# State-space tables from TensorE outer products, their products on GpSimd, and another merged step order

## The chip, the cores and the metric

One core of a Trainium2 chip runs the whole program. The metric is the device time of one execution in microseconds. Three timed runs of the kernel before took 551.61, 553.63 and 553.75 us; the median is 553.63.

## The reference

The input is `x`, four batches of 512 tokens with 128 features. One layer is computed for each batch, in four parts.

1. Cross attention with 16 heads of 8 over a context of 77 keys, with an output projection and a residual sum.
2. A mixture of 8 experts (128 to 512 to 128, ReLU). A router picks two experts for each token, but all eight are computed and the unused ones weigh zero.
3. A text block: four heads of scores over the 77 keys, of which only the 32 largest of each row are kept (top-32), a softmax on those, a FiLM scale and shift made from the result, a state-space convolution over the 512 tokens (S4D), a second FiLM and a feed-forward part.
4. An 8-bit quantised 128 by 128 product with residual sum at the end.

The S4D convolution needs a kernel K of 512 time steps for each of the 128 channels. It does not depend on `x`:

```python
dt = exp(log_dt);  A = A_re + 1j*A_im;  dtA = dt[:, None] * A
dC = C * (exp(dtA) - 1) / A
powers = exp(dtA[:, :, None] * arange(L))
K = 2 * einsum('dn,dnl->dl', dC, powers).real        # 128 channels, 64 states
y = irfft(rfft(x) * rfft(K))[:L] + x * D_skip
```

## The kernel before

Everything is float32 except a few bf16 pieces of the attention scores. Every engine walks one list, `order`, and executes its own part of each step in that order. Semaphores join the engines. `order` is made in `plan()` from eleven streams of steps and the string `ORDER`, a hand-stored merge: each letter names a stream, with a repeat count. The streams: S setup, H attention and router of batches 0 to 3, K the S4D kernel tables, F FiLM weights, E expert products (`moe_up`, `moe_down`), C the sums of expert outputs (`moe_add`), U and T the text block, O the convolution, feed-forward and quantisation, Z the second half of that for the last batch, W warming matmuls that compute nothing needed. The E steps of a batch can start once its normalised tokens are transposed (`norm_T` of `moe`). The text block of a batch starts after its expert sums, and the last batch's text block has no expert products left beside it.

PSUM has eight banks. Four belong to the experts (`moe_h`, `moe_y`). The other four, `side`, are handed out in turn by `place_fills` in the order of the list, so a product cannot start until the reader of the fourth fill before it has emptied that bank. From the first to the last step of an attention group, its accumulator holds one of the four, and three rotate.

The stream K builds the tables of K. Partitions are 64 states, twice (real and imaginary); time is split as l = 32a + c, with a in 0..15 and c in 0..31.

- `kgen_base` 0 (VectorE, L1525 to L1539) makes the per-channel decay and angle, `ar`, `r`, `u32`, `a32`. `kgen_base` 1 (L1543 to L1569, with a Tanh and two Sin on ScalarE) makes the coefficients `p1` and `p2`.
- The channels then go in four groups of 32. For group i, `kgen_ang` (VectorE, L1577 to L1584) makes the angles 32a, sine and cosine, as a broadcast product and range reductions by adding and subtracting a large number, on 128x512 elements. `kgen_rot` (L1589 to L1592) does the same for the angles c on 128x1024. `kgen_sin` is three Sin on ScalarE.
- `kgen_exp` is two broadcast products on GpSimd (L1756, L1757) and two Exp on ScalarE, into the single buffers `G1d` and `G2c`.
- `kgen_mul` is five products or sums on VectorE (L1598 to L1603), `t1` to `t4` on 512 columns and `tab` on 1024.
- `kgen_mm` is 32 small matmuls on TensorE (L1023), waiting for `tab`; ScalarE copies the result.

After the fourth group `kgen_dft` transforms K. The first step that needs the result belongs to the text block of batch 0. `setup_used` makes VectorE and GpSimd wait for early setup data, whose memory the tables overlay.

Other names: `attn_norm` (L872 on TensorE; reciprocal L1322 and product L1324 on VectorE), `o_proj` (L879, sum L1328), the LayerNorm steps `ln_stats` (L1276 to L1283, reciprocal root on GpSimd L1640) and `ln_apply` (L1293), `score` and `pv` (L850, L854, L865, exponential L1112), `smax` (L834, L1311), `topk` (L1384 to L1394) and `topw`.

Of the kernel before, what the change touches and what calls it, by code (L numbers as in the profile page):

```python
# [7 lines left out]
ALU = mybir.AluOpType  # L8
# [49 lines left out]
C_COLS = [("ident", 128), ("spread", HG * HD0), ("sign", 1), ("cosoff", 1), ("sinoff", 1), ("p1sign", 1), ("cvec", CC), ("avec", CA),  # L58
          ("half", 2), ("rest", NM), ("rest_on", NM), ("ones", 2)]
# [141 lines left out]
S H2 S H5 K H2 K W2 F2 W2 F W2 F W6 F H3 K H K2 H2 W K H2 K H18 K8 H W K H2 K H2 K3 H E10 H E6 H2 K E2 K H C2 K E6 K  # L201
E4 H C H2 E3 H E K2 C H E H E2 K2 E7 C E2 H2 E H C E H E3 H E C E H E2 C E4 H E2 C E U E7 C H E3 U H2 U H14 U H2 T H
C H2 E T H E5 T E5 H E C E7 H E C H C H E T E2 H E3 H2 E C2 E H E2 U3 H3 E11 C H T2 U T E H E3 C H T2 E3 C H2 E5 T
E3 T C T E H E4 H E2 H E3 C H E2 H C E2 U H E T E T3 E7 H2 T E H U T C T H3 T E H E H9 C H E T H T H2 T4 H E H2 T E6
C2 T H E4 O H U H2 E4 H E2 C H E H E3 H U C E2 U O E7 U H C E H T2 C O T E10 H2 E2 H O E O C E T E3 O2 U C U E U E2
H E U E T E H2 O C H U T3 E O2 E H E C E5 C E H E O E H T E4 T H E4 C2 E H E3 T E T E6 C T2 H E H E2 C E H2 T H E U
H2 E H E T E2 T7 H O E H3 T H2 E2 H E2 T H3 E H C E2 O E T H O E T H2 C2 T U2 O E H E3 U O E2 U E3 T H C E9 O T H E
C2 E T H2 T2 E6 C E8 O H2 C2 E H E O H T E T E2 H E5 T U O2 C U E12 O C E U2 E T O U T U T2 C E T4 E C O E2 T E5 T5
E2 T O2 C O T E11 C2 E8 T E C E3 O E2 T E T O E3 T C O E O E2 C O2 E U2 E2 C U E3 U E4 O E T E C T O E O E7 C O T O
E5 C O E T E C T O C U3 T4 U O T2 W U T7 O T O U T6 W O W T3 W O6 W7 O3 Z O Z W Z2 O2 Z O Z O3 Z2 O W2 Z2 O Z2 O Z O  # L210
Z
# [129 lines left out]
def plan():  # L341
# [3 lines left out]
    for run in ORDER.split():  # L345
        name = run[0]
        for _ in range(int(run[1:] or 1)):
# [12 lines left out]
         "dft": 2, "idft": 1, "ffn_up": HC, "ffn_down": 1, "quant_T": 1, "quant_mm": 1, "kgen_mm": 1, "kgen_dft": 2}  # L360
# [4 lines left out]
def place_fills(order):  # L365
# [13 lines left out]
    for kind, b, i in order:  # L379
# [8 lines left out]
        if kind == "attn_sum":  # L388
# [20 lines left out]
G_ACT = ["dt", "th", "sh", "sb"] + [(n, i) for i in range(ND) for n in ("s1", "s2", "s3", "e1", "e2")]  # L409
# [6 lines left out]
def recurrent_layers(nc, x, w1, w2, wpack, vpack, cpack, rpack, gpack, r2pack, xpack, vctx, dftf, dfti, b2, tmask, vmask, out):  # L416
# [10 lines left out]
    with ExitStack() as ctx:  # L427
# [7 lines left out]
        AREA = 13440  # L435
# [1401 lines left out]
```

## Time and profile before

| | |
|---|---|
| median of three timed runs | 553.63 us |
| profiled execution | 553.78 us, span 552.0 us |
| TensorE matmul busy | 478.6 us (87%), 2883 instructions |
| VectorE busy | 430.9 us (78%) |
| ScalarE busy | 264.7 us (48%) |
| GpSimd busy | 117.0 us (21%) |
| mean granted TensorE clock | 0.933 of full speed |
| the chain that ended last | 70% PE, 22% VectorE, 3% ScalarE, 2% GpSimd |
| first expert product (L910) starts; last expert product ends | 102.9 us; 468.0 us |
| last expert sum (L1370) starts | 469.65 us |

The span runs from the first to the last instruction; the execution's own time is 1.8 us longer. Busy shares are averages over stages that have different limits. The chain is followed back from the last instruction, at each step to what released it, so that its shares say which engine the end depended on. A matmul's end is modelled from a pipeline, and neighbouring ones overlap by some tenths of a microsecond; in the chain that overlap is taken out. The granted clock of TensorE has two levels here, 2.4 GHz (1.00) and 1.2 GHz (0.5); a mean between them is a mixture.

### The profile page before, as it was taken

The numbers are of one execution on the slowest core, as the hardware profiler recorded it, in microseconds if no ns is written. First come the engines' busy times: TensorE is split into PE (matmuls) and PEld (weight loads), VectorE is DVE, ScalarE is ACT, GpSimd is POOL, SyncE is SP. The second block draws the span as 40 slices with busy tenths as digits, with TensorE's granted clock in tenths as the row PEclk, the third lists the DMA queues.
The fourth block names the chain that finished last, engine by engine and source line by source line (L and its number), as shares of the span: only waits on it lengthen the run. The fifth ranks groups of instructions, "written<-read, shape, count | busy, mean of one in ns | idle before, by whom it ended". The sixth has DMA issues, their size and how long they took to land.

```text
span 552.0 us, 8986 instructions
## 1 busy us (share of the span) xinstructions
PE 478.6 (87%) x2883; PEld 370.6 (67%) x2883; DVE 430.9 (78%) x1781; ACT 264.7 (48%) x549; POOL 117.0 (21%) x198
## 2 busy tenths in 40 slices
PE   4386586799999999999999999999999999736971
PEld 3154234598975989848987985689878989514760
DVE  4378988885625787886797988899898789998667
ACT  4441466575456465564538456534474544411040
POOL 4522003122020031003015210310222331232021
PEclk9998595699999999999999999999999999956996
DMA  7900770002100004000003000000000000000000
GB/s 182 173 2 0 222 220 0 2 1 39 21 2 2 1 1 58 4 1 1 2 0 51 9 4 1 2 20 0 2 2 1 2 20 1 1 1 0 21 0 19
DMA packets 16176, 15.03 MB, mean 27 GB/s; under 512 B 1210, under 2 KB 14274, under 8 KB 16130
## 3 DMA queue, kind: packets, MB, share of 16 engines
q1 hardware_dynamic: 16130, 14.47, 11.7%
q8 instruction: 23, 0.38, 0.3%
q14 instruction: 23, 0.19, 0.1%
HBM read 9.15 MB, written 1.05 MB: 18 GB/s over the span
## 4 chain that ended last, share of the span: by engine, by line
PE 70%; DVE 22%; ACT 3%; issue 3%; POOL 2%; DMA 1%; DVEq 0%; POOLq 0%; ACTq 0%
PE moe_h L910 20%; PE moe_y L922 20%; PE side L865 5%; PE side L970 3%; PE side L980 2%; PE side L958 2%; DVE area L1394 2%; PE moe_h L932 2%; PE side L1001 2%; PE side L772 2%; DVE TOP L1384 1%; PE side L944 1%; PE side L989 1%; PE side L834 1%; PE side L1023 1%
## 5 line engine op out<-in xcount | busy, mean ns | idle before, releaser
L1132 ACT ACTIVATE HT<-moe_h,W 128x256 f32<-128x256 f32 x256 | 115.5, 473 | 104.0 <-PE moe_h L910 103.8
L910 PE MATMUL moe_h<-xnT_moe,W 128*128 128x256 f32 x512 | 138.0, 387 | 0.8 <-ACT HT L1132 0.7
L922 PEld LDWEIGHTS moe_y<-W,HT 128*128 128x128 f32 x1024 | 131.3, 192 | 8.8 <-issue 3.2
L922 PE MATMUL moe_y<-W,HT 128*128 128x128 f32 x1024 | 134.9, 276 | 0.0
L910 PEld LDWEIGHTS moe_h<-xnT_moe,W 128*128 128x128 f32 x512 | 88.3, 193 | 17.8 <-issue 7.2
L1370 DVE SCALAR_TENSOR_TENSOR X<-moe_y,RW,X 128x128 f32<-128x128 f32 x128 | 38.9, 346 | 8.1 <-PE moe_y L922 7.1
L865 PE MATMUL side<-PT,VP 128*72 128x512 f32 x80 | 43.1, 625 | 1.2 <-ACT PT L1112 1.2
L1394 DVE MATCH_REPLACE8 area<-TOP,area 128x77 f32<-128x77 f32 x192 | 40.9, 230 | 0.0
L932 PE MATMUL moe_h<-W 128*128 128x256 f32 x112 | 31.7, 436 | 0.0
L1384 DVE MAX8 TOP<-area 128x8 f32<-128x77 f32 x192 | 31.5, 230 | 0.0
L1704 POOL TENSOR_TENSOR area<-area 128x128 f32<-128x128 f32 x16 | 7.4, 463 | 110.3 <-ACT area L1155 110.3
L932 PEld LDWEIGHTS moe_h<-W 128*128 128x128 f32 x112 | 24.6, 223 | 9.2 <-issue 5.7
L1112 ACT ACTIVATE PT<-side 128x512 f32<-128x512 f32 x40 | 23.3, 594 | 13.5 <-PE side L850 10.6
L1311 DVE TENSOR_REDUCE mx<-side 128x6 f32<-128x462 f32 (+1 forms) x48 | 24.8, 580 | 5.7 <-PE side L834 5.6
L1384 DVE MAX8 TOP<-side 128x8 f32<-128x77 f32 x64 | 10.8, 231 | 17.4 <-PE side L945 17.3
L958 PE MATMUL side<-FF,AMT 78*128 78x512 f32 x32 | 19.4, 693 | 4.2 <-ACT AMT L1149 4.2
L1146 ACT ACTIVATE area<-area 128x308 f32<-128x308 f32 x16 | 7.4, 460 | 30.6 <-DVE area L1387 30.6
L834 PE MATMUL side<-KM,QA 96*128 96x154 bf16 x128 | 12.3, 237 | 10.5 <-DMA QA<-Q 9.8
L865 PEld LDWEIGHTS side<-PT,VP 128*72 128x72 f32 x80 | 11.1, 150 | 13.3 <-issue 8.2
L834 PEld LDWEIGHTS side<-KM,QA 96*128 96x128 bf16 x128 | 9.6, 100 | 14.8 <-DMA QA<-Q 11.4
L850 PE MATMUL side<-QA,KM 128*128 128x512 bf16 x32 | 12.7, 410 | 7.8 <-issue 6.8
L1756 POOL TENSOR_TENSOR area<-area,C 128x512 f32<-128x512 f32 x4 | 4.2, 1054 | 68.8 <-PE side L1023 51.8
(323 smaller groups left out, 851.8 us busy)
## 6 DMA issues: line engine op xcount, KB each, us to landing
W<-in_w SPq DMA_DIRECT2D x8, 512.0 KB, 7.7
QA<-Q SPq DMA_DIRECT2D x24, 128.0 KB, 4.4
X<-in_x SPq DMA_DIRECT2D x4, 256.0 KB, 6.5
KM<-area SPq DMA_DIRECT2D x6, 160.0 KB, 5.9
out_dram<-FO SPq DMA_DIRECT2D x3, 256.0 KB, 2.3
V<-in_vpack SPq DMA_DIRECT2D x1, 579.0 KB, 7.7
area<-in_r2pack SPq DMA_DIRECT2D x1, 576.0 KB, 8.0
area<-in_gpack SPq DMA_DIRECT2D x1, 576.0 KB, 8.5
```

The costliest lines, as they stand in the source:

```text
L834: mm = pe.matmul(dst[:, o:o + 2 * NK], QA[0:ZROWS, j, i * P:(i + 1) * P], KM[0:ZROWS, j, b, 0:2 * NK], start=True, stop=True)
L865: mm = pe.matmul(dst[0:GROWS, :], VP[:, g, n, :], PT[:, i % NPT, :], start=(n == 0), stop=(n == NG - 1))
L910: pe.matmul(moe_h[n % 2][:, 0:HS], W1[:, e, c * P:(c + 1) * P], xnT_moe[:, b % 2, h * HS:(h + 1) * HS], start=True, stop=True).then_inc(mo ...
L922: mm = pe.matmul(moe_y[m % 2][:, t * P:(t + 1) * P], HT[:, m % 2, c, t * P:(t + 1) * P], W2[:, e, c, :], start=(c == 0), stop=(c == HC - 1))
L932: pe.matmul(moe_h[n % 2][:, 0:HS], W[:, 0:P], W[:, 0:HS], start=True, stop=True)
L958: pe.matmul(dst[:], AMT[:, i % 2, :], FF[:, b, :], start=True, stop=True).then_inc(full, 1)
L1112: act.activation(PT[:, i % NPT, :], src[:], ACT.Exp).then_inc(read, 1)
L1132: act.activation(HT[:, m % 2, c, :], moe_h[n % 2][:, 0:HS], ACT.Relu, bias=wc("b1")[:, e * HC + c:e * HC + c + 1]).then_inc(moe_h_ready, 1)
L1311: dve.tensor_reduce(mx[:, i, :].rearrange("p (u j) -> p j u", u=2)[:, 3 * n:3 * n + pairs, :], src[:, 0:heads * NK].rearrange("p (j u k) - ...
L1370: ins = dve.scalar_tensor_tensor(X[:, b, t, :], moe_y[m % 2][:, k * P:(k + 1) * P], RW[:, b % 2, t, e:e + 1], X[:, b, t, :], ALU.mult, ALU ...
L1384: dve.max(TOP[:, a, h, r, :], s).then_inc(top_max, 1)
L1394: dve.match_replace(TW[:, h, :], TOP[:, a, h, r, :], s, PICKED)\
```

## The change

The broadcast products leave VectorE and GpSimd. A new step `kgen_T` transposes `u32`, `r`, `a32` and `ar` on TensorE into one bank, and ScalarE copies it to `UT`. A constant matrix `ES` (32 rows, 512 columns with a and 1024 with c, block diagonal over the 32 channels of a group) is loaded four times, by four DMAs on SyncE, behind `gpack`. The angles and exponents of a group are then products of 32 rows of `UT` with `ES` into PSUM: one matmul of 512 columns for `kgen_ang`, two for `kgen_rot`, three for `kgen_exp`. VectorE rounds straight from PSUM in four operations of 512 columns for `kgen_ang` and four for `kgen_rot`; the Sin takes a negative scale and a bias column. The Exp reads PSUM, as one operation for `G1d` and two for `G2c`. The five operations of `kgen_mul` run on GpSimd. They wait for `p2`, the Sin and the Exp. TensorE's `kgen_mm` now waits for GpSimd; VectorE's `kgen_ang` and `kgen_rot` of groups 2 and 3 wait for GpSimd's `t4` and `tab` of the group two before.

`kgen_base` 1 moves behind the first group's Sin in stream K. `ORDER` is another merge throughout: 82 steps stand before the first `moe_up` in both. Between the first `moe_up` and the last `moe_down` stand 754 steps before and 755 after: `kgen_rot` of group 3, and `topk` (1, 0), `topw` 0 and `text_n4` 0 of the last batch come in, and `ln_stats`, `ln_apply` and `norm_T` of `ffn` of batch 2 go behind the last `moe_down`. `topk` (1, 1) of the last batch now also stands before the last `moe_add`.

```diff
+    out = [("kgen_base", 0, 0), ("kgen_T", 0, 0)]
     for dh in range(ND + 1):
         if dh < ND:
             out += [("kgen_ang", 0, dh), ("kgen_rot", 0, dh), ("kgen_sin", 0, dh)]
+        if dh == 0:
+            out.append(("kgen_base", 0, 1))
...
-S H2 S H5 K H2 K W2 F2 W2 F W2 F W6 F H3 K H K2 H2 W K H2 K H18 K8 H W K H2 K H2 K3 H E10 H E6 H2 K E2 K H C2 K E6 K
+S H2 S H5 W5 K F3 K H3 W F2 H K3 W4 H2 K2 W4 H6 K H11 K H6 K8 H K2 H3 K H E4 H K4 H E2 K H E4 K H E H E C H E7 H K E
...
+            for g in range(ND):
+                sp.dma_start(ES[DH * g:DH * (g + 1)], epack).then_inc(e_in, 16)
...
+                if kind == "kgen_T":
+                    dst, full = free_for(pe, kind, b, i)
+                    pe.wait_ge(g_dve, GD["a32"])
+                    for n, k in enumerate(("u32", "r", "a32", "ar")):
+                        mm = pe.transpose(dst[:, n * P:(n + 1) * P], ga[k][:], ident)
+                    mm.then_inc(full, 1)
+                if kind in ("kgen_ang", "kgen_rot", "kgen_exp"):
+                    g = slice(DH * i, DH * (i + 1))
...
+                    for n, (k, c) in enumerate({"kgen_ang": ((0, 0),), "kgen_rot": ((1, 1), (1, 2)),
+                                                "kgen_exp": ((2, 0), (3, 1), (3, 2))}[kind]):
+                        dst, full = free_for(pe, kind, b, i, n)
+                        pe.matmul(dst[:], UT[g, k * P:(k + 1) * P], ES[g, c * 512:(c + 1) * 512], start=True, stop=True,
+                                  tile_position=(DH * i, 0)).then_inc(full, 1)
                 if kind == "kgen_mm":
-                    pe.wait_ge(g_dve, GD["tab", i])
+                    pe.wait_ge(g_pool, GP["tab", i])
...
                 if kind == "kgen_exp":
-                    act.wait_ge(g_pool, GP["m1", i])
-                    act.activation(G1d[:], G1d[:], ACT.Exp).then_inc(g_act, 1)
-                    act.wait_ge(g_pool, GP["m2", i])
-                    act.activation(G2c[:], G2c[:], ACT.Exp).then_inc(g_act, 1)
+                    if i == 0:
+                        setup_used(act)
+                    if i >= 1:
+                        k, m = FILL[("kgen_mm", 0, i - 1, 0)]
+                        act.wait_ge(side_full[k], m + 1)
+                    src, read = filled(act, kind, b, i, 0)
+                    act.activation(G1d[:].rearrange("p d a -> p (d a)"), src[:], ACT.Exp).then_inc(read, 1)
+                    for n in range(2):
+                        src, read = filled(act, kind, b, i, n + 1)
+                        act.activation(G2c[:].rearrange("p d c -> p (d c)")[:, n * 512:(n + 1) * 512], src[:], ACT.Exp).then_inc(read, 1)
...
                 if kind == "kgen_ang":
...
+                    if i >= 2:
+                        dve.wait_ge(g_pool, GP["t4", i - 2])
+                    src, read = filled(dve, kind, b, i)
+                    dve.tensor_scalar(G1b, src[:], cc("cosoff"), ROUND, ALU.add, ALU.add).then_inc(g_dve, 1)
+                    gelem(("y1", i), dve.tensor_scalar(G1c, src[:], cc("sinoff"), ROUND, ALU.add, ALU.add))
+
+                    dve.scalar_tensor_tensor(G1b, G1b, ROUND, src[:], ALU.subtract, ALU.subtract).then_inc(g_dve, 1)
+                    dve.scalar_tensor_tensor(G1c, G1c, ROUND, src[:], ALU.subtract, ALU.subtract).then_inc(read, 1)
...
-                if kind == "kgen_exp":
-                    a32 = ga["a32"][:, DH * i:DH * (i + 1)].unsqueeze(2).broadcast_to((P, DH, CA))
...
-                    gelem(("m1", i), pool.tensor_tensor(G1d[:], a32, av, ALU.mult))
-                    gelem(("m2", i), pool.tensor_tensor(G2c[:], a1, cv, ALU.mult))
+                if kind == "kgen_mul":
...
+                    pool.wait_ge(g_dve, GD["p2"])
+                    pool.wait_ge(g_act, GA["s2", i])
+                    gelem(("t1", i), pool.tensor_tensor(G1b[:], G1b[:], p1, ALU.mult))
+                    gelem(("t2", i), pool.tensor_tensor(G1c[:], G1c[:], p2, ALU.mult))
+                    gelem(("t3", i), pool.tensor_tensor(G1b[:], G1b[:], G1c[:], ALU.add))
+                    for n in range(3):
+                        emptied(pool, "kgen_exp", 0, i, n)
+                    gelem(("t4", i), pool.tensor_tensor(G1d[:], G1d[:], G1b[:], ALU.mult))
+                    gelem(("tab", i), pool.tensor_tensor(G2c[:], G2c[:], G2b[:], ALU.mult))
```

## Rows read from the trace of the kernel before

**Rows 1.** Stages (window, its length, busy us with instructions per engine; granted clock; DMA).

```profile
47.00:82.00 35.00, 22.27 (x135) 9.41 (x133) 32.42 (x48) 16.43 (x26) 2.96 (x2) 0.76 0.57 174
82.00:103.00 21.00, 12.32 (x99) 9.36 (x97) 17.49 (x28) 12.14 (x21) 6.97 (x5) 0.51 0.00 0
103.00:135.00 32.00, 31.18 (x284) 26.42 (x285) 22.10 (x57) 22.85 (x47) 6.10 (x10) 0.95 0.02 4
135.00:468.00 333.00, 333.00 (x2059) 270.12 (x2058) 267.64 (x1258) 176.63 (x391) 65.09 (x119) 1.00 0.06 10
468.00:504.00 36.00, 20.92 (x77) 12.05 (x76) 33.88 (x211) 10.57 (x24) 11.56 (x19) 0.74 0.00 1
504.00:552.00 48.00, 30.47 (x147) 23.42 (x146) 31.30 (x106) 7.87 (x16) 7.83 (x11) 0.86 0.04 12
```

**Rows 2.** Chain that ended last, 80 to 99 us (start us, us, what).

```profile
80.01 2.15 PE side L1023 x64
...
83.78 3.37 DVE qr L1322
...
94.30 1.05 POOL rstd_moe L1640
...
95.38 3.71 DVE xn_head L1293 x4
```

**Rows 3.** VectorE timeline (start us, us, engine, line): first coefficient operation, and what follows them.

```profile
36.51 0.22 DVE L1543 TENSOR_SCALAR area<-area 128x128 f32<-128x128 f32 x1
...
44.80 0.29 DVE L1514 TENSOR_REDUCE area<-area 128x1 f32<-128x128 f32 x1
```

**Rows 4.** VectorE timeline: one round of angles, rotations and products.

```profile
60.76 0.69 DVE L1577 TENSOR_TENSOR area<-area,C 128x512 f32<-128x512 f32 x1
...
61.49 0.49 DVE L1579 TENSOR_SCALAR area<-area,C 128x512 f32<-128x512 f32 x1
...
64.91 1.23 DVE L1589 TENSOR_TENSOR area<-area,C 128x1024 f32<-128x1024 f32 x1
...
68.94 0.69 DVE L1598 TENSOR_TENSOR area<-area 128x512 f32<-128x512 f32 x1
...
73.11 0.69 DVE L1577 TENSOR_TENSOR area<-area,C 128x512 f32<-128x512 f32 x1
```

**Rows 5.** ScalarE timeline: first score exponential, last copy of attention, a table load.

```profile
63.13 1.08 ACT L1112 ACTIVATE PT<-side 128x512 f32<-128x512 f32 x2
...
79.26 0.59 ACT L1118 ACTIVATE qs<-side 64x512 f32<-64x512 f32 x1
...
84.26 1.28 ACT L1179 ACT_TABLE_LOAD   x1
```

**Rows 6.** PE: 128x512 float32 product in the chain, 34 to 104 us.

```profile
38.52 0.86 PE side L807 x2
```

**Rows 7.** PE timeline of the scores: such a product at the lower clock.

```profile
66.04 1.91 PE L865 MATMUL side<-PT,VP 128*72 128x512 f32 x2
```

**Rows 8.** VectorE timeline: a sum that reads 512 columns of PSUM.

```profile
91.94 0.69 DVE L1328 TENSOR_TENSOR X<-side,X 128x512 f32<-128x512 f32 x1
```

**Rows 9.** GpSimd timeline beside the LayerNorm of the chain.

```profile
95.70 1.05 POOL L1756 TENSOR_TENSOR area<-area,C 128x512 f32<-128x512 f32 x1 [0.36 <-PE side L1023]
...
96.83 1.91 POOL L1757 TENSOR_TENSOR area<-area,C 128x1024 f32<-128x1024 f32 x1
```

**Rows 10.** GpSimd, the line of a plain 128x512 sum: ns min/median/max.

```profile
L1670 POOL TENSOR_TENSOR FO<-FO,xn_out x3: 1270/1272/1272, 362.8 to 511.1; 128x512 f32<-128x512 f32 x3
```

**Rows 11.** VectorE timeline: the same LayerNorm line with GpSimd idle.

```profile
122.96 1.12 DVE L1293 TENSOR_SCALAR xn_head<-X,mv_attn,rstd_attn 128x128 f32<-128x128 f32 x4 [0.68 <-POOL rstd_attn L1640]
```

**Rows 12.** VectorE timeline, top-32 rounds of the last batch.

```profile
472.60 0.67 DVE L1384 MAX8 TOP<-side 128x8 f32<-128x77 f32 x4
...
474.55 0.65 DVE L1384 MAX8 TOP<-area 128x8 f32<-128x77 f32 x4
...
475.94 0.65 DVE L1384 MAX8 TOP<-area 128x8 f32<-128x77 f32 x4
```

More of the change, by code:

```diff
@@ L359 @@
          "score": 1, "attn_norm": 1, "o_proj": 1, "router": 1, "w_T": 1, "b2_add": 1, "text_q": 1, "topk": 1, "am_T": 1, "film": 1,
-         "dft": 2, "idft": 1, "ffn_up": HC, "ffn_down": 1, "quant_T": 1, "quant_mm": 1, "kgen_mm": 1, "kgen_dft": 2}
+         "dft": 2, "idft": 1, "ffn_up": HC, "ffn_down": 1, "quant_T": 1, "quant_mm": 1, "kgen_mm": 1, "kgen_dft": 2,
+         "kgen_T": 1, "kgen_ang": 1, "kgen_rot": 2, "kgen_exp": 3}
 SIDE = 4
@@ L390, in place_fills @@
     return where
-K_DVE = {"kgen_ang": ("y0", "x1", "x2", "x", "y1", "y2", "y"), "kgen_rot": ("e0", "e1", "e3", "e2"),
-         "kgen_mul": ("t1", "t2", "t3", "t4", "tab")}
 G_RHS = ["ra0", "ra1", "ra2", "rf", "rf2", "rs"]
-G_DVE = (["ar", "ai", "u", "uk", "r", "u32a", "u32k", "u32", "a32", "d1", "d2", "d3", "dd", "om", "om2",
-          "em", "cb1", "cb", "nr0", "nr", "ni", "z1", "z2", "z3", "zr", "z4", "z5", "z6", "zi",
+G_ANG = ["x1", "y1", "x", "k0", "k1"]
+G_DVE = (["ar", "ai", "u", "uk", "r", "u32a", "u32k", "u32", "a32", "d1", "d2", "d3", "dd"]
+         + [(n, 0) for n in G_ANG] + ["om", "om2", "em", "cb1", "cb", "nr0", "nr", "ni", "z1", "z2", "z3", "zr", "z4", "z5", "z6", "zi",
           "c1", "c2", "c3", "p1", "c4", "c5", "c6", "p2"]
-         + [(n, i) for kind, _, i in kernel_steps() for n in K_DVE.get(kind, ())]
+         + [(n, i) for i in range(1, ND) for n in G_ANG]
          + [("ks", 0), ("ks", 1), "kd", "kd0", "spec"])
 G_POOL = (["f1", "f2", "f3", "f4", "b1", "b2", "b3", "b4", "b5", "b6", "m1", "m2"]
-          + [(n, i) for i in range(ND) for n in ("m1", "m2")] + ["skip"])
+          + [(n, i) for i in range(ND) for n in ("t1", "t2", "t3", "t4", "tab")] + ["skip"])
 GD = {name: n + 1 for n, name in enumerate(G_DVE)}
@@ L406, with recurrent_layers @@
 GP = {name: n + 1 for n, name in enumerate(G_POOL)}
[L409 removed]
+G_ACT = ["dt"] + [(n, 0) for n in ("s1", "s2", "s3")] + ["th", "sh", "sb"] + [(n, i) for i in range(1, ND) for n in ("s1", "s2", "s3")]
 GA = {name: n + 1 for n, name in enumerate(G_ACT)}
 LN_KINDS = ["attn", "moe"] + TEXT + ["ffn", "out", "quant"]
[L416 removed]
+def recurrent_layers(nc, x, w1, w2, wpack, vpack, cpack, rpack, gpack, r2pack, xpack, vctx, dftf, dfti, b2, tmask, vmask, epack, out):
     order = plan()
@@ L432, in sem @@
             return ctx.enter_context(nc.semaphore(name))
-        AREA = 13440
+        AREA = 13952
         area = sb("area", [P, AREA])
@@ new lines, in _ @@
+                if kind == "kgen_rot":
+                    G2b = G2b2[i % 2].rearrange("p d c -> p (d c)")
+                    if i >= 2:
+                        dve.wait_ge(g_pool, GP["tab", i - 2])
+                    for n in range(2):
+                        src, read = filled(dve, kind, b, i, n)
+                        dve.tensor_scalar(G2b[:, n * 512:(n + 1) * 512], src[:], cc("cosoff"), ROUND, ALU.add, ALU.add).then_inc(g_dve, 1)
+                    for n in range(2):
+                        src, read = bank(kind, b, i, n), side_read[FILL[(kind, b, i, n)][0]]
+                        dve.wait_ge(g_dve, GD["k%d" % n, i])
+                        dve.scalar_tensor_tensor(G2b[:, n * 512:(n + 1) * 512], G2b[:, n * 512:(n + 1) * 512], ROUND, src[:],
+                                                 ALU.subtract, ALU.subtract).then_inc(read, 1)
@@ L1819 @@
                             np.tile(np.arange(CC), (P, 1)), np.tile(np.arange(CA), (P, 1)),
+                            np.where(top, 0.25 * TWO_PI, 0.0)[:, None], np.where(top, 0.0, 0.25 * TWO_PI)[:, None],
                             (p[:, None] >= NK) == np.arange(2), rest, rest & (p[:, None] % 32 < KR_),
@@ L1825 @@
            "b2": a["L0_ffn_b2"], "tmask": a["mask_BxS_bf1"].view(np.uint8).reshape(B * T, P).T,
-           "vmask": a["mask_BxS2_bf1"].view(np.uint8).reshape(1, B * NK)}
+           "vmask": a["mask_BxS2_bf1"].view(np.uint8).reshape(1, B * NK),
+           "epack": np.concatenate([np.kron(np.eye(DH), np.arange(n)[None]) for n in (CA, CC)], 1).astype(np.float32)}
     nc = bacc.Bacc("TRN2", target_bir_lowering=False, num_devices=1)
```

84 lines of the change are left out of this document (29 added, 55 removed).

## The prediction

> **What bounds the kernel now.** I read first the table by stages [rows 1]. From 103 us, where the expert products begin, to 468 us, where they end, PE has work almost without a break, 31.18 of 32 us and 333.00 of 333 us, at a clock of 0.95 and then 1.00: the sum of PE work sets this stage, and anything taken from VectorE there gives nothing by itself. Before it, from 47 to 103 us, PE is busy for 34.6 of 56 us, at clocks of 0.76 and 0.51, while VectorE is busy for 49.9 us. After it, from 468 to 504 us, VectorE has 33.88 of 36 us, and it sets the stage. From 504 us on the end is a chain of short dependent steps. So there are three places: a head that VectorE sets, a middle that PE sets, and a tail that VectorE sets and then latency.
>
> The chain in order of time shows the end of the head [rows 2]: the small matmuls of group 0, which wait for VectorE's table (80.01), the reciprocal of the attention norm (83.78), GpSimd's root (94.30), and a LayerNorm of 3.71 us (95.38). Between these stand VectorE operations of the stream K, in the queue ahead of what the chain needs. The expert products then begin at 102.9 us.
>
> **The work that moves.** One round on VectorE takes, by the starts in [rows 4], 4.15 us of angles (60.76 to 64.91), 4.03 us of rotations and 4.17 us of products: 12.35 us, and 49.4 us for the four groups. After the change it has eight operations of 512 columns from PSUM. A sum of that shape that reads PSUM takes 0.69 us [rows 8]; a scalar operation on SBUF takes 0.49 us [rows 4]. Eight are 3.9 to 5.5 us. I take 5.1, near the PSUM row, as all eight read PSUM. VectorE loses 7.3 us a group, 29 us in all. In front of the first `moe_up` it had three rounds of angles and rotations and two of products, 32.9 us, and now has three at 5.1, so 17.6 us less.
>
> GpSimd loses 1.05 + 1.91 us a group [rows 9] and gains three operations of 512 without a broadcast or two of them, one of 1024. The broadcast form is 1.05 us, the plain form 1.27 us [rows 10]; two, two, and about 2.4 for the 1024 (1.27 doubled, less a fixed part) make 7.0, with gaps 7.4 us, 30 us in all. GpSimd was at 21%, so its sum doesn't matter, only its latency does.
>
> PE gains six matmuls of 512 float32 columns a group. One takes 0.86 us at full clock [rows 6] and 1.7 to 1.9 us at the lower one [rows 7]. Four groups are 20.6 us at full clock, with the four transpositions some 21 us. Of these, group 3's rotation (2) and exponent (3) stand behind the first `moe_up`, 5 x 0.86 = 4.3 us; the rest stand in the head.
>
> **Head, up to the scores.** The coefficients take 8.3 us of VectorE (36.51 to 44.80) [rows 3] and stood before the row maxima that the scores need. They now stand behind them. Group 0's rotation (2.5 us) comes in front of them instead, and its angles shrink by 1.6 us: 7.4 us less in that queue. Against it: TensorE holds `kgen_T` in front of the first `smax`, so that waits for `a32`; each PSUM fill adds a handoff; four warming steps stand between the rotation's fills and the last `smax`. I take 2.9 us for these (bounds 1 and 6), which leaves 4.5 us. Behind the maxima ScalarE now has Tanh, Sin and Exp of the coefficients and of group 0, with three table loads of 1.28 us [rows 5], in front of the first score exponential: some 6.5 us. About as much lay there before (the DMA of the maxima, group 0's last Sin and a load), so I keep the gain and round it to 4.9 us: the first exponential comes at 58.2 in place of 63.13 [rows 5]. The four added DMAs (0.79 MB) stand on SyncE behind `gpack`, with some 5 us free before the next issue there, and cost nothing as the first `smax` now waits for `kgen_T` anyway; if they delayed the query pieces by more than 5 us, the head would lose the excess.
>
> **Head, scores.** Ten pairs of score and value products run from 63.13 to the last copy at 79.26 [rows 5], 16.1 us. Three outer products between them add 2.6 us. `attn_norm` no longer stands behind `kgen_mm` of group 0 (2.15 us [rows 2], and its wait for the table), so that it starts at the copy and not at 82.1: 2.9 us less. The first three pairs ran at the lower clock, at 1.91 us where the full clock needs about 1; with exponents and warming steps just ahead of them PE may come in at full clock. I take half of the 2.7 us, 1.4.
>
> **Head, norm to experts.** Call the end of `attn_norm` on PE T, 83.7 us before. From there to the first expert product took 19.2 us. After the change PE has, in this order, `kgen_mm` 0 (2.15), three fills for exponent 1, three for angles and rotation 2 (5.2 at full clock), and only then `o_proj`. The fills wait for banks: ScalarE must first finish Sin 1, copy `kgen_mm` 0, load a table and do the exponents, to about T + 6.7. So `o_proj` ends near T + 9, where the reciprocal and product were ready at T + 4.1. VectorE does angles and rotation 2 meanwhile, to T + 10.3, in the place of products 1 that took 4.2 us, then the residual sum and statistics to T + 12.6. GpSimd's `t4` and `tab` of group 1 start at T + 6.7 and end at T + 10.4, ahead of the root, which ends at T + 13.7. The LayerNorm then meets `t1` to `t3` of group 2. It took 3.71 us beside GpSimd's two operations [rows 2, 9] and takes 1.12 with GpSimd idle [rows 11]; each GpSimd operation held one of its four instructions. I keep 3.7. Then `kgen_mm` 1 and exponent 2 (both in front of `norm_T` on PE, and exponent 2 in front of its copy on ScalarE), the transposition, angles 3, router: the first `moe_up` at T + 21, bounds 19 and 25. That costs 1.8 us.
>
> The Trainium skill (SBUF — State Buffer, Who interferes with whom) says that VectorE and GpSimd share one port pair by an exclusive lock, and that a VectorE instruction contends when it is in a 2-port mode or has two SBUF inputs. The LayerNorm rows agree for the first case. By that rule the rounding operations, which read PSUM, stay free beside GpSimd, and the attention product `OT` times `OV`, with two SBUF inputs, could wait up to one GpSimd operation more, 1.3 us, at a place where `o_proj` waits for PE in any case. The rule speaks against moving 30 us of work to GpSimd, and puts the LayerNorm at 3.7 us or more.
>
> Head in all: -4.9 + 2.6 - 2.9 - 1.4 + 1.8 = -4.8 us.
>
> **Middle.** +4.3 us of PE work, in the stage where it adds fully. Of the 32 us at clock 0.95 [rows 1], a tenth ran at half clock; I take 0.6 off for a warmer entry. `kgen_mm` 2 and 3 now wait for GpSimd: group 2's `tab` ends near T + 22, before PE reaches it past four expert steps and two fills, and group 3's has some 3 us to spare. If that cover is gone PE waits for the whole shortfall, up to 3 us. The exchange of a few text steps changes the sum by tenths. Middle: +3.7 us.
>
> **Tail.** At the last expert sum VectorE has two top-32 rounds of the last batch already behind it, 472.60 to 475.94 in [rows 12], 3.3 us, and the work of 12 us of removed tables gave room for them. But the second half's first score product comes by a path (LayerNorm, transposition behind `ffn_up`, projection, product) of some 9 us, beside which only about 7.5 us of VectorE work is left: 1.5 us are given back. Tail: -1.8 us; zero to -3.3 as bounds.
>
> **Sum.** 552.0 - 4.8 + 3.7 - 1.8 = 549.1 us of span. With the 1.8 us around it, as in the profiled execution (553.78 for 552.0, 0.15 above the median of 553.63), 550.9. That is the forecast, 2.7 us, just under 0.5%, below the median.
>
> **Rivals.**
> 1. *The head stays warm.* PE has 17 us more work between 33 and 103 us. If this keeps its clock at 1.00 where it was 0.76 and 0.51 [rows 1], transposition, router, `o_proj` and the first expert steps save half their time: about 2 more in the scores' first pairs, 1 in transposition and router, 1.5 at the entry. 546 us. For it: the two idle stretches ahead of both falls were waits for VectorE. Against it: bank waits leave idle stretches of the same kind.
> 2. *Fills at the lower clock in front of the chain (slower).* The clock at T is 0.51, as now. Then six fills between T and `o_proj`, and three in front of `norm_T`, cost 1.7 instead of 0.86 us, and `kgen_mm` 1.5 more each: some 5 to 6 us on the chain, which eat the head's gain; the middle adds its 4.3 with no relief, and the tail gives nothing, as VectorE arrives late. 552 + 4.3 + 0.5 + 1.8 = 558.5 us. [...]
> 3. *Nothing in the sum.* The head gives 4.5, the middle takes 4.5, the tail gives under one: 553.3. For it: the middle has no free PE time at all.
> 4. *The new merge has waits of its own* in 365 us of expert stage, where before there were none of length. At 1% that is 3.6 us: 555 us. Nothing in a profile of before speaks on it; it shares the chance of rival 2.
>
> **Chances.** Forecast 0.34; rival 1, 0.22; rival 3, 0.16; rivals 2 and 4, 0.28. A time differs from no change when it is off by more than 0.5%, 2.8 us, so under 550.9 or over 556.4. Rival 1 and a good half of the forecast lie below, 0.40; of rivals 2 and 4 a share of 0.24 lies above; 0.36 is left between. The range that leaves 0.1 on either side is 543.5 to 559; it covers the bounds of the head (+6 and -5 us) and of the tail. The likeliest case's own is 548.5 to 553.
>
> **What would show it.** The first score exponential near 58 us and the first L910 line near 98 us; a PE wait of any length for GpSimd at `kgen_mm` would be wrong. VectorE's busy time near 402 us, PE's near 500, GpSimd's near 134. The LayerNorm ahead of the experts at 3.7 us. The expert stage, first `moe_up` to last `moe_down`, near 369 us where it was 365. The last expert sum to the last instruction, 82.4 us now, near 80.5. The forecast is wrong if the head gains under 2 or over 8 us, or the expert stage grows by more than 6 or shrinks.

## The result and the profile after

The changed kernel takes 572.22 us (median of 4 runs, 569.91 to 573.81) against 553.69 for the kernel before on the same chip: ratio 1.0338, 95% interval 1.0293 to 1.0384. It is slower by 3.4%, where 550.9 us was forecast and the range ended at 559. The profiled execution took 572.81 us with a span of 570.9; before it was 552.0, so 18.9 us are to be found.

The table by stages, kernel after (columns as in [rows 1]; the last product of the experts ends at 487 instead of 468, so that the ends of the last three windows are moved by 18 or 19):

```profile
47.00:82.00 35.00, 32.96 (x158) 16.33 (x157) 19.11 (x41) 18.73 (x30) 7.00 (x5) 0.88 0.59 174
82.00:103.00 21.00, 21.00 (x98) 11.22 (x96) 13.05 (x24) 13.41 (x23) 13.26 (x11) 0.51 0.00 1
103.00:135.00 32.00, 32.00 (x198) 22.57 (x197) 11.79 (x42) 15.38 (x29) 10.28 (x7) 0.68 0.00 1
135.00:487.00 352.00, 349.70 (x2159) 281.06 (x2162) 272.64 (x1290) 184.00 (x409) 65.17 (x124) 1.00 0.06 10
487.00:523.00 36.00, 19.20 (x79) 11.13 (x78) 33.66 (x197) 11.80 (x25) 13.05 (x21) 0.76 0.00 0
523.00:570.00 47.00, 33.62 (x151) 26.36 (x149) 28.40 (x95) 7.11 (x14) 7.62 (x11) 0.79 0.04 12
```

Two columns changed. VectorE's 32.42 and 17.49 us of the first two windows [rows 1] are 19.11 and 13.05: the table work did leave it. PE's 22.27 and 12.32 are 32.96 and 21.00: from 82 to 135 us PE never rests. And in the third window, where the experts run, PE was busy 31.18 of 32 us at a clock of 0.95 for 284 instructions; now it is busy all 32 us at 0.68 and gets through 198.

The same stretch cut where the granted clock changes (the last number but two is the clock), kernel after:

```profile
72.00:81.00 9.00, 9.00 (x57) 3.07 (x56) 3.72 (x5) 5.18 (x9) 0.00 (x0) 1.00 0.51 142
81.00:84.00 3.00, 3.00 (x37) 1.91 (x35) 2.97 (x2) 2.96 (x7) 1.69 (x2) 0.74 0.00 0
84.00:108.00 24.00, 24.00 (x108) 13.67 (x106) 15.04 (x41) 12.35 (x20) 13.85 (x10) 0.50 0.00 1
108.00:114.00 6.00, 6.00 (x73) 3.95 (x72) 3.22 (x6) 4.20 (x8) 1.15 (x2) 0.78 0.00 0
114.00:126.00 12.00, 12.00 (x29) 6.95 (x30) 0.94 (x3) 6.89 (x14) 5.84 (x4) 0.50 0.01 1
126.00:129.00 3.00, 3.00 (x18) 2.68 (x18) 0.77 (x2) 0.22 (x2) 0.00 (x0) 0.86 0.00 0
```

And the kernel before, same view:

```profile
84.00:105.00 21.00, 12.32 (x93) 10.10 (x93) 19.19 (x30) 11.60 (x18) 5.38 (x4) 0.50 0.00 0
105.00:108.00 3.00, 2.91 (x11) 1.67 (x11) 2.83 (x10) 1.88 (x5) 0.00 (x0) 0.76 0.00 0
108.00:135.00 27.00, 26.27 (x271) 23.36 (x270) 17.34 (x47) 19.55 (x41) 6.10 (x10) 1.00 0.02 5
```

Before, the clock is at its lower level (0.50, 1.2 GHz) from 84 to 105 us, while PE works for 12.32 of 21 us, and comes back to 1.00 (2.4 GHz) in the first 5 us of the expert products. The fall itself is no new thing: in both kernels it comes at 81 to 84 us (0.76 before, 0.74 after) with PE busy for 3.00 of 3 us. What is new is what follows: after, the clock stays down for 24 us with PE busy in all of them, rises for a moment and falls again for 12. What PE does there is in the chain of waits, kernel after (start us, us, what):

```profile
79.93 2.13 PE side L1044 x64
82.06 7.77 PE side L1038 x11
89.83 2.00 PE side L884 x8
91.84 3.53 PE side L1044 x64
95.36 5.41 PE side L1038 x6
100.78 1.05 PE side L777 x4
101.82 2.00 PE side L1038 x2
103.82 1.81 PE side L890 x8
105.63 0.63 PE moe_h L915
```

L1038 are the new outer products (32 rows of 128, 512 columns). The number behind the x counts instructions, and a float32 product is two of them here, for the outer products as for the products of the experts and the warming steps. The whole chain between attention and experts, which was VectorE, GpSimd and PE in turn [rows 2], is now PE alone, and 15.2 of its 25.7 us are outer products: three of them (x6) take 5.41 us here, where three take 3.11 us at 42.46 us. The first expert product starts at 105.5 us; 98 was forecast.

Earlier, on PE and ScalarE ahead of the first score (timeline, kernel after):

```profile
54.47 2.10 PE L1038 MATMUL side<-area 32*128 32x512 f32 x3
56.49 6.40 PE L937 MATMUL moe_h<-W 128*128 128x256 f32 x16
62.95 0.38 PE L855 MATMUL side<-QA,KM 128*128 128x512 bf16 x1
...
66.16 1.12 PE L1038 MATMUL side<-area 32*128 32x512 f32 x2
...
73.00 1.98 PE L1038 MATMUL side<-area 32*128 32x512 f32 x4
...
59.01 1.08 ACT L1211 ACTIVATE area<-side 128x512 f32<-128x512 f32 x2
63.15 1.08 ACT L1133 ACTIVATE PT<-side 128x512 f32<-128x512 f32 x2 [3.05 <-remote]
```

The exponents of group 0 are done at 60.1 us. The first score product then waits behind four warming steps, which take 6.40 us, most of it at the lower clock; the same sixteen instructions take 3.62 us at a clock of 1.00 (e7 below, at 54.11 us). The clock of after over the warming steps at 45.50 us and at 56.49 us, each behind three outer products:

```profile
45.00:48.00 3.00, 3.00 (x7) 2.05 (x7) 2.97 (x6) 1.33 (x2) 0.00 (x0) 0.50 0.00 0
57.00:60.00 3.00, 3.00 (x8) 2.36 (x7) 2.42 (x9) 2.97 (x6) 0.00 (x0) 0.50 0.94 290
```

From 42 to 45 us it was 0.98. The first exponential is at 63.15, where 63.13 was before [rows 5] and 58.2 was forecast. The two later rows of L1038 rule out that a product on 32 rows is slow by itself: between score products, at a clock of 1.00, one takes 1.12 us and two take 1.98, where 128-row ones take 1.02 and 1.91 in the same places (e1).

### The profile page after: what moved, and what is told of

The parts are those of the page before. It is cut to its first block, busy times and chain, and to the rows that moved or that the text cites. A ratio compares the mean times of both kernels' runs of the same rounds, so it can differ in the third digit from the quotient of the medians.

```text
span 570.9 us, 9092 instructions
## 1 busy us (share of the span) xinstructions
PE 521.0 (91%) x2929; PEld 388.8 (68%) x2935; DVE 404.6 (71%) x1749; ACT 269.5 (47%) x556; POOL 132.4 (23%) x210
## 3 DMA queue, kind: packets, MB, share of 16 engines
HBM read 9.93 MB, written 1.05 MB: 19 GB/s over the span
## 4 chain that ended last, share of the span: by engine, by line
PE 76%; DVE 14%; ACT 4%; issue 3%; POOL 1%; DMA 1%; another core or an unknown queue 1%; ACTq 0%; DVEq 0%; POOLq 0%
PE moe_y L927 19%; PE moe_h L915 19%; PE side L870 6%; PE side L1038 5%; PE side L975 3%; PE side L963 2%; PE moe_h L937 2%; PE side L994 2%; PE side L777 2%; DVE area L1425 2%; PE side L1044 2%; PE side L1006 2%; PE side L985 2%; PE side L839 1%; PE side L949 1%
## 5 line engine op out<-in xcount | busy, mean ns | idle before, releaser
L927 PEld LDWEIGHTS moe_y<-W,HT 128*128 128x128 f32 x1024 | 133.4, 194 | 11.1 <-issue 5.2
L915 PE MATMUL moe_h<-xnT_moe,W 128*128 128x256 f32 x512 | 139.8, 391 | 0.7 <-ACT HT L1153 0.5
L927 PE MATMUL moe_y<-W,HT 128*128 128x128 f32 x1024 | 136.4, 278 | 0.0
L870 PE MATMUL side<-PT,VP 128*72 128x512 f32 x80 | 41.0, 602 | 0.8 <-ACT PT L1133 0.6
L937 PE MATMUL moe_h<-W 128*128 128x256 f32 x112 | 34.1, 464 | 0.0
L1038 PE MATMUL side<-area 32*128 32x512 f32 x48 | 32.8, 888 | 0.0
L937 PEld LDWEIGHTS moe_h<-W 128*128 128x128 f32 x112 | 26.3, 240 | 8.8 <-issue 4.5
L1662 POOL TENSOR_TENSOR rstd_text<-ve_text,minus_half 128x2 f32<-128x2 f32 x8 | 6.0, 751 | 69.2 <-DVE ve_text L1314 69.1
L975 PE MATMUL side<-area,FW 128*128 128x256 f32 x80 | 20.4, 412 | 0.0
L1038 PEld LDWEIGHTS side<-area 32*128 32x128 f32 x48 | 11.0, 258 | 13.8 <-issue 11.2
```

Of the source, the lines that this page charges most:

```text
L870: mm = pe.matmul(dst[0:GROWS, :], VP[:, g, n, :], PT[:, i % NPT, :], start=(n == 0), stop=(n == NG - 1))
L915: pe.matmul(moe_h[n % 2][:, 0:HS], W1[:, e, c * P:(c + 1) * P], xnT_moe[:, b % 2, h * HS:(h + 1) * HS], start=True, stop=True).then_inc(mo ...
L927: mm = pe.matmul(moe_y[m % 2][:, t * P:(t + 1) * P], HT[:, m % 2, c, t * P:(t + 1) * P], W2[:, e, c, :], start=(c == 0), stop=(c == HC - 1))
L937: pe.matmul(moe_h[n % 2][:, 0:HS], W[:, 0:P], W[:, 0:HS], start=True, stop=True)
L975: mm = pe.matmul(dst[:, q * 2 * D:(q + 1) * 2 * D], FW[:, k, (2 * n + q) * P:(2 * n + q + 1) * P], src[:, k::2, :], start=(k == 0), stop=( ...
L1038: pe.matmul(dst[:], UT[g, k * P:(k + 1) * P], ES[g, c * 512:(c + 1) * 512], start=True, stop=True, tile_position=(DH * i, 0)).then_inc(ful ...
```

## The experiments

Each column is read from the profiled execution: the start of the first expert product, the start of the last, and the difference, the stage of the experts. Each ratio is to executions of the kernel before that belong to that row; their medians were 553.7 us for after, 554.1 for the next three rows, 555.7 for products on GpSimd, for old middle with 128 rows and for bf16, and 553.8 for the other two.

| Kernel | first | last | stage | mean clock | median us | ratio, 95% |
|---|---|---|---|---|---|---|
| before | 102.8 | 467.9 | 365.1 | 0.933 | 553.7 | |
| after | 105.5 | 487.3 | 381.8 | 0.913 | 572.2 | 1.034 (1.029 to 1.038) |
| 128 rows | 101.9 | 477.0 | 375.1 | 0.943 | 559.3 | 1.009 (1.004 to 1.013) |
| merge only | 113.6 | 492.9 | 379.3 | 0.920 | 576.2 | 1.039 (1.033 to 1.045) |
| tables only | 129.8 | 497.2 | 367.4 | 0.901 | 582.8 | 1.049 (1.044 to 1.054) |
| before, products on GpSimd | 102.4 | 476.3 | 373.9 | 0.914 | 562.7 | 1.013 (1.009 to 1.017) |
| old middle, 32 rows | 104.4 | 482.1 | 377.7 | 0.911 | 568.3 | 1.023 (1.018 to 1.027) |
| old middle, 128 rows | 96.4 | 463.3 | 366.9 | 0.961 | 559.1 | 0.995 (0.990 to 1.000), four fastest of ten; see text |
| 128 rows, bf16 | 94.3 | 469.6 | 375.3 | 0.936 | 554.3 | 0.998 (0.995 to 1.001) |
| old middle, 128 rows, warm moved | 101.5 | 468.4 | 366.9 | 0.941 | 553.6 | 1.000 (0.996 to 1.003) |

From the last expert product to the end it is 84.1 us before and 83.6 after, so nothing of the difference lies in the tail. (The others take 83.0 to 84.2, but for 80.5 with the merge only and 87.3 with the warming moved.)

**e1: the outer products on 128 rows.** My theory was the clock: PE busy with 32-row products leaves it at the lower level. The rival was plain PE time.

```
-  pe.matmul(dst[:], UT[g, k * P:(k + 1) * P], ES[g, c * 512:(c + 1) * 512],
-            start=True, stop=True, tile_position=(DH * i, 0)).then_inc(full, 1)
+  pe.matmul(dst[:], UTs[i][:, k * P:(k + 1) * P], ES[:, c * 512:(c + 1) * 512],
+            start=True, stop=True).then_inc(full, 1)
   # UTs: four buffers, zero but for the 32 rows of their group
```

> The changed kernel, in which each outer product reads all 128 rows and not 32: the transposed table is copied once per group with zeros in the other rows (four copies of 32 rows on ScalarE, zeroed by GpSimd early on), and the columns, the order and the waits stay. The changed kernel took 572.2 us; its clock is 0.50 from 83 to 126 us, over products of 32 rows that keep PE busy without a gap. Theory A, products on 32 of the 128 rows don't hold the clock up: here it stays near 1.00 from 83 us on, the stretch from 82 to 105 us shrinks by some 7 us and the expert stage by some 11 us; 555 to 561 us. Theory B, the new merge's own order and waits cost the time: no change, 570 to 574 us. Theory C, the products' PE time itself, whatever their rows: no change either.

559.32 us, 13 us less than after, with the same count and width of products. By stages, kernel with 128 rows:

```profile
75.00:84.00 9.00, 9.00 (x74) 5.58 (x74) 4.05 (x2) 7.36 (x13) 3.98 (x4) 0.62 0.01 2
84.00:90.00 6.00, 4.90 (x77) 3.72 (x76) 5.83 (x10) 2.96 (x4) 3.56 (x2) 0.97 0.01 3
90.00:105.00 15.00, 11.55 (x28) 6.91 (x28) 10.25 (x31) 6.03 (x13) 8.01 (x6) 0.61 0.00 1
105.00:108.00 3.00, 3.00 (x9) 1.31 (x9) 0.75 (x1) 2.59 (x5) 0.00 (x0) 0.73 0.00 0
108.00:135.00 27.00, 27.00 (x258) 22.98 (x258) 12.65 (x35) 16.35 (x35) 11.39 (x14) 1.00 0.20 27
```

The clock still falls at 75 us, behind products of 8 rows and 64 instructions of 16 columns, but beside the 128-row products it is back at 84. It doesn't stay there: from 90 to 105 us it is 0.61, with PE idle for 3.45 us of them, so that the part of the expectation that wanted it near 1.00 from 83 us on failed. From 108 us on it is 1.00, as before, where after had 0.78 and then 0.50 until 126. And the two falls of after at 45 and 57 us are gone, in e1 as in e7 (from 42 to 75 us both have 1.00), while e9, with 32 rows, has them (0.54 from 45 to 48 us, 0.68 from 57 to 60):

```profile
42.00:75.00 33.00, 30.09 (x113) 14.77 (x112) 21.99 (x47) 19.83 (x32) 7.00 (x5) 1.00 0.63 184
```

That is the line of e1. Of the 10.9 us between the two profiled executions 3.6 are in the head and 6.7 in the stage of the experts. The theory's main claim holds, that 32-row products leave PE at the lower clock; what is left against before, 10 us in the stage, is all but 0.5 us not the clock's (its half-rate time there is 2.4 us by the windows, 1.8 before).

**e2: the other way round, the kernel before with its warming products on 32 rows.**

```
-  pe.matmul(moe_h[n % 2][:, 0:HS], W[:, 0:P], W[:, 0:HS], start=True, stop=True)
+  pe.matmul(moe_h[n % 2][:, 0:HS], W[0:DH, 0:P], W[0:DH, 0:HS], start=True, stop=True)
```

> The kernel before, in which the warming matmuls (which compute nothing needed) read 32 rows and not 128, with the same columns. Theory A: the clock is lower than before in the stretches that they fill (31 to 47 us, 525 us on): it falls to 0.5 within 33 to 47 us, where it was 1.00, and the total rises by 1 to 5 us. Theories B and C: the clock and the time stay as they were, 552 to 555 us.

570.78 us (one run) against 554.12. PE timeline, that kernel:

```profile
37.57 3.77 PE L932 MATMUL moe_h<-W 32*128 32x256 f32 x8
...
48.82 10.60 PE L932 MATMUL moe_h<-W 32*128 32x256 f32 x24
...
76.58 1.95 PE L865 MATMUL side<-PT,VP 128*72 128x512 f32 x2 [0.85 <-ACT PT L1112]
...
80.18 1.02 PE L865 MATMUL side<-PT,VP 128*72 128x512 f32 x2
```

And the kernel before, same view:

```profile
36.63 1.89 PE L932 MATMUL moe_h<-W 128*128 128x256 f32 x8
...
41.80 5.34 PE L932 MATMUL moe_h<-W 128*128 128x256 f32 x24
```

Eight such instructions take 3.77 us in place of 1.89, and the 24 take 10.60 in place of 5.34, though both read as many columns. PE worked for 34.06 us from 28.9 to 63, and everything in it ran at half rate, the 128-row products of L807 too (1.99 us at 41.27, where the kernel before has 1.02 at 38.36). In the kernel before the first eight, at 29.89 us, took 3.71 us as well; the next were at full rate. Here PE reached full rate at 80 us, in the scores, which work on 128 rows. The first expert product came at 115.2 instead of 102.8. The recorded clock reads 1.00 all this time, against the durations. So in this trace the record can't be trusted until its first change. My expectation of a visible fall in the record was wrong for this reason.

**e3 and e4: the new merge alone, the new tables alone.**

```
e3:  before, with the order table, kernel_steps() and the split of kgen_base of after
e4:  after, with the order table of before and kgen_base 1 ahead of kgen_T
```

> The new merge alone: steps in the order of the changed kernel, with the coefficients behind the first group's Sin, but the tables computed as before (angles, rotations and products on VectorE, exponents on GpSimd, no outer products; the transposing step is empty). Theory B: the loss is here, 565 to 575 us. Theories A and C: no outer products, so no loss of that kind; with VectorE carrying 29 us more than the merge was fitted to, 552 to 560 us.

> The new tables alone: outer products, rounding from PSUM and products on GpSimd, in the merge and stream order of before, with the transposing step just ahead of the first angles. Theories A and C: 565 to 575 us, as the same 48 matmul passes of 32 rows stand in the same stage; by A the clock is at 0.50 over most of 83 to 120 us. Theory B: under 558 us.

576.22 and 582.78 us, both above every range that was expected. Neither half stands alone. e3 had been put at 565 to 575 us by the theory that the merge is the loss; but in it PE waits for tables that VectorE still has to make (waits; us in total, times, longest), where the kernel after has no wait of this kind:

```profile
PE side L1025 <- DVE area L1605: 23.7, 3, 9.0
```

With the new tables in the old merge the outer products stand in front of the scores: the score exponentials start from 64.7 to 85.8 us, where before had them from 63.1 to 76.8, and the experts start at 129.8. The clock is 0.50 from 90 to 129 us there, as theory A expected. So the merge had to be fitted, and the pair gives no size for a part of the 18.9 us.

**e5: only the products to GpSimd, everything else as before.**

```
-K_DVE = {..., "kgen_mul": ("t1", "t2", "t3", "t4", "tab")}
+K_POOL = {"kgen_exp": ("m1", "m2"), "kgen_mul": ("t1", "t2", "t3", "t4", "tab")}
```

> The kernel before with one part of the change alone: the five products of each group run on GpSimd (with the same waits on p2, Sin and Exp, and VectorE's angles and rotations of groups 2 and 3 waiting for the products of two groups before); angles, rotations, exponents and the merge stay as before, so no outer products. If the products on GpSimd were a part of the loss (their 7.4 us a group in place of 4.2, and the LayerNorm held by them), 555 to 560 us. If the outer products and the merge alone were, VectorE's chain up to the experts loses 8.4 us of queue and the first expert product comes 2 to 6 us earlier than 102.9: 548 to 553 us.

562.70 us: 7 us slower than the 555.66 of the kernel before beside it, with the experts starting when they did (102.4) and their stage 8.8 us longer. Timelines of that kernel in the stage of the experts, where the next batch's LayerNorm runs:

```profile
127.37 4.90 DVE L1293 TENSOR_SCALAR xn_head<-X,mv_attn,rstd_attn 128x128 f32<-128x128 f32 x4 [0.69 <-POOL rstd_attn L1633]
...
127.31 1.06 POOL L1757 TENSOR_TENSOR area<-area 128x512 f32<-128x512 f32 x1
128.45 1.06 POOL L1758 TENSOR_TENSOR area<-area 128x512 f32<-128x512 f32 x1
129.58 1.26 POOL L1759 TENSOR_TENSOR area<-area 128x512 f32<-128x512 f32 x1
130.93 1.26 POOL L1761 TENSOR_TENSOR area<-area 128x512 f32<-128x512 f32 x1
...
132.42 1.04 PE L772 MATMUL side<-C,xn_head 128*128 128x128 f32 x4 [3.13 <-DVE xn_head L1293]
```

Each of the four LayerNorm instructions ends with one GpSimd product: 4.90 us where the same line took 1.12 [rows 11], and PE, which has the transposition next, waits 3.13 us. With another 1.97 us on a ScalarE result PE idles 5.4 us in a stage that had 0.8. The other 4 us are about what the lower clock costs, 0.81 from 102.4 to 135 us where before had 0.94; no run separates the two. This collision is one of order: in after this LayerNorm (131.5 us) meets no product and takes 1.12 us for the four. The Trainium skill (SBUF — State Buffer, Who interferes with whom) has this as an exclusive lock on a shared port pair; the rows agree, down to the pairing of the ends.

**e9 and e7: the old middle.** Both take the new order only as far as the step that makes the spectrum, and from there on the steps in the order of before; e9 with the 32-row products of after, e7 with 128 rows.

```
ORDER = after's order up to ("kgen_spec", 0, 0), then before's order of the steps that are left
```

> The 128-row version of the changed kernel (559.3 us) with its own merge only up to the end of the tables (126 steps), and behind that the steps in the order of before. If the new merge has waits of its own in the expert stage (it took 375.2 us there against 365.1, of which five outer products explain 4.3), the stage shrinks to 368 to 371 us and the time to 553 to 556. If the rest of the 10 us comes from the tables in that stage (fills, banks, GpSimd), it stays at 558 to 561.

> The kernel after, its 32-row outer products and GpSimd products kept, with the new order only up to the step that makes the spectrum of the state-space tables and from there the steps in the order of the kernel before. The stage of the experts was 381.9 us after and 365.1 before; the kernel with 128 rows took 375.4 with the new order and 367.2 with the old one. Theory (the loss is the clock, and beside it the new order of the middle costs 6 to 8 us): about 6 us less than after, 564 to 567, stage of the experts 374 to 377, first UP product still at 104 to 107 and the clock at its lower level until 120 or later. Rival (the order of the middle costs nothing by itself, the stage with 128 rows and the new order was longer through its clock alone): 570 to 574, stage about 381.

e9 took 568.27 us, 4 less than after and just above the 564 to 567 of the theory; the stage of the experts gave 4.1 (377.7 for 381.8); its clock over the stretch in question:

```profile
81.00:126.00 45.00, 44.84 (x204) 25.49 (x204) 20.14 (x50) 23.97 (x42) 20.52 (x16) 0.50 0.00 1
126.00:129.00 3.00, 3.00 (x19) 2.61 (x18) 0.00 (x0) 0.95 (x2) 1.44 (x1) 0.80 0.00 0
```

45 us at 0.50 with PE busy for 44.84 of them. The one difference to e7 is the rows of the outer products, and in e7's profiled execution, one of the two fastest of ten, the window looks so:

```profile
42.00:135.00 93.00, 84.10 (x599) 56.57 (x598) 57.63 (x130) 58.91 (x106) 33.91 (x30) 1.00 0.29 75
```

93 us at 1.00, though PE is idle for 9 of them; the experts start at 96.4 and the stage takes 366.9, a little less than the 368 to 371 expected. That execution took 549.41 us, where 553 to 556 was expected. But of ten executions two took 549 us, two 555 to 556 and six 559 to 560, and the mean clock falls with the time from 0.961 to 0.935. The same program differs by 10 us from one execution to the next, and its mean clock with it; where the clock is lower in the slower ones isn't shown, as none of them was profiled. Even the slowest stays 6 us under the fastest of e9 (565.96).

**e8: bf16 operands for the 128-row products** (the tables' angles and exponents are rounded to bf16, which changes what is computed).

> The 128-row version of the changed kernel, in which both operands of the outer products are bf16, which changes the computation: angles and exponents are rounded to bf16. A product is then one pass of 512 columns in place of four, some 0.22 us in place of 0.86. By PE time: 0.64 us less for each of the 5 products in the expert stage, which gives 3.2 us there, and up to 19 x 0.64 = 12 us less of PE work in the head, of which a part is hidden: 549 to 556 us. If PE time of the products no longer counts once the clock is up: 558 to 560 us.

554.32 us, 5 less than e1, and in the profiled executions 7.2 less, all before the experts (94.3 for 101.9). So the time of the outer products counts in the head, 7.6 us of at most 12. The 3.2 us expected of the stage did not come: it stays at 375.3. By the windows its half-rate time is 4.4 us against 2.4 in e1, and PE waits 1.4 us longer in it, which is about what the shorter products save; this is a reckoning, not an experiment.

**e10: the warming steps ahead of the first score moved into PE's later waits.**

```
-... ("kgen_exp", 0, 0), ("warm", 0, 10) to ("warm", 0, 13), ("score", 0, 0) ...
+... ("kgen_exp", 0, 0), ("score", 0, 0) ...    one in front of kgen_mm 1, three in front of norm_T
```

> The kernel with 128-row outer products and the old order of the middle, with the four warm steps that stood ahead of the first score moved: one to the wait ahead of the second spectrum product (PE idle 2.0 us there), three to the wait ahead of the LayerNorm transposes of the experts (PE idle 3.5 us there). If those warm steps (3.6 us on PE, 54.1 to 57.7) hold up the scores, the first exponential of the scores comes 2 to 3.6 us earlier than 58.5 and the first UP product as much, 94 instead of 96.4, and the time of an execution without a dip of the clock is 546 to 548. If the scores wait for data and not for PE, nothing moves: 549 for the best and about 558 for most executions. If the four steps also keep the clock up between smax and the scores, it falls there and the time is 556 to 562 throughout.

```profile
50.66 2.74 PE L1030 MATMUL side<-area 128*128 128x512 f32 x6
56.85 0.39 PE L847 MATMUL side<-QA,KM 128*128 128x512 bf16 x1 [3.45 <-ACT area L1202]
58.41 1.95 PE L862 MATMUL side<-PT,VP 128*72 128x512 f32 x2 [1.17 <-ACT PT L1124]
```

The score waits for the exponents of group 0 (L1202), not for PE: the first exponential comes 0.9 us earlier than in e7, where 2 to 3.6 were expected. The first pairs then run at the lower clock (1.95 us for the first value product, 1.05 in e7), and the experts start at 101.5. 553.62 us, range 551.5 to 558.5 (the profiled execution took 557.61): steadier than e7 and no better than before. No version here beats the kernel before by more than the measurement tells.

## Why the prediction was wrong

The 18.9 us: the experts start 2.7 us later, their stage is 16.7 us longer, and from its last product to the end it is 0.5 shorter. Of the 16.7, 4.3 are the forecast outer products at full clock. From the granted clocks of the windows above, the half-rate time from 105.5 to 129 us costs 2.5 x 0.50 + 6 x 0.22 + 12 x 0.50 + 3 x 0.14 = 9.0 us, where before it cost 2.2 x 0.50 + 3 x 0.24 = 1.8: 7.2 more. That leaves 5.2 us for the new order of the middle. The two pairs that differ in that order give much the same once their clocks are taken out in the same way: after against e9 is 4.1 us, but e9 lost 11.4 us to the clock and after 9.0, so 6.5; e1 against e7 is 8.2 us, of which 2.4 are the clock's, so 5.8. Of these 5 to 6.5 us only 1.5 are PE's idle time (2.3 us in the stage after, 0.8 before); the rest stays open.

Step by step:
- *The work that moves*: right. VectorE 404.6 us busy (402 forecast), GpSimd 132.4 (134). PE 521.0, not 500: the count was right, for the kernel with 128 rows has 502.0; the other 19 us come with the lower clock of 32 rows.
- *Head, up to the scores* (forecast -4.9): failed, measured 0. (The text's own terms gave 4.5; the 4.9 has no reason of its own.) The group's fills ended, and the four warming steps ran, at the lower clock. With 128 rows the first exponential is at 58.9, close to the 58.2.
- *Head, scores*: right, and a little better: from there to the end of `attn_norm` 16.8 us (18.9 forecast), all at full clock.
- *Head, norm to experts* (T + 21, bounds 19 and 25): failed, T + 25.6. T itself is 79.9 us and the clock was at 1.00 there, which the forecast wanted. I took the queue of six and three fills as the forecast has them, but at 0.86 us a product (two instructions of the trace); they took 1.3 to 1.8, and what stands between them ran at half rate too. The LayerNorm beside GpSimd was right (3.81 us, forecast 3.7).
- *Middle* (+3.7): failed, +16.7. The "warmer entry" of -0.6 was a colder one of +7.2, and the new order, which the forecast put at nothing and rival 4 at 3.6, cost 5 to 6.5.
- *Tail* (-1.8): failed. From the last expert sum to the end it is 83.0 us, where it was 82.4 and 80.5 was forecast. No run here was made on it.

Rival 2 had the place and the kind, fills at the lower clock in front of the chain, but its condition did not hold, and its price was too low. It had the clock at its lower level already at T, as before, and gave the middle its 4.3 us and nothing for the clock; the clock was at 1.00 at T, PE then did not wait at all (21.00 of 21 us from 82 us on), and the clock stayed down until 20 us into the experts. Rivals 2 and 4 together, 558.5 + 3.6 = 562.1, are still 10 us short. The failed step, in the forecast as in rival 1, is that the added work counts as any PE work: it was priced at full clock behind T, and taken to help the clock ("a warmer entry"). Nothing in [rows 1 to 12] showed an operation on 32 rows at length, and I took its clock and duration from a 128-row one ([rows 6]: 77 columns of weights, 128 rows), without a bound for the other case.

The Trainium skill (TensorE: Matmul & The Clock Gate, Part 1: The HAM clock gate) says that the gate follows how busy PE has been. By busy time alone the windows of after at 84 to 108 us would be at 2.4 GHz. They are at 1.2 GHz with PE busy throughout; the measurement decides.

Shown by experiment: the rows of the outer products, 13 us (e1) and 9 by the medians of e7 and e9 (19 by the two profiled executions); that products on 32 rows leave PE at half rate in another kernel too (e2, one execution); that the new order of the middle costs (4.1 us by e9, 8.2 with 128 rows by e1 and e7). Argued from the windows only: the 7.2 us for the clock in the stage, and with it the 5 to 6.5 of the order. Open: why the clock falls at 75 us in e1 and not in e7, with the same PE work in front of it; and what the new order costs beyond its 1.5 us of idle time.

## What to carry to other kernels

Here products on 32 of the 128 rows filled PE's time, and the clock stayed down beside them, or fell behind three of them: moving cheap work to an idle PE in this form can slow everything behind it. The same products over 128 rows, zeros in 96 of them, cost no PE time more (1.02 us against 1.12, both at 1.00) and brought 13 us back. So an idle engine's free time isn't all that counts; what form the work has there counts too. Before pricing work at PE's full clock, look for a row of the same shape in the trace, and where there is none, bound it at half rate, its neighbours included. Work given to GpSimd must be placed so that it doesn't run beside VectorE's LayerNorm: the four instructions took 4.90 us instead of 1.12.

## What the runs showed of the hardware that was not expected

- Beside float32 products of 32 rows the granted clock stayed at 0.50 for 45 us with PE busy for 44.84 of them (e9), and eight warming instructions took 3.77 us on 32 rows against 1.89 on 128 (e2).
- In e1 the products multiply zeros in 96 of their 128 rows, and the clock, once fallen, is back at 84 us after 9 us (until 90 us), where in after it stayed down for 24.
- The recorded clock can read 1.00 from the start and be wrong until its first change: in e2 products run at half rate from 30 to 79 us under a recorded 1.00.
- One program's executions differ by 10 us (549.3 to 560.0, e7), and their mean granted clock with it (0.961 to 0.935).
